# Cross attention of an audio tower: which engine subtracts the maximum from which unit, and ScalarE instructions over two PSUM banks

## The chip, the core and the metric

The kernel runs on one core of a Trainium2 chip. The metric is the device time of one execution in microseconds; the time before is the median of three runs. A core has TensorE (matmuls, from SBUF into PSUM), VectorE, ScalarE and GpSimd, which run side by side, each through its own list of instructions in order, and wait for one another by semaphores. PSUM has banks of 512 fp32 values for each of 128 partitions.

## What is computed

The program is five stages: choice of tokens, retention, a mixture of experts, cross attention, a second mixture of experts. The change touches cross attention alone. Its reference, with 4096 tokens of text (8 batches of 512), 128 videos of 64 frames and 2 heads of 64:

```
q = (text_embeds @ Wq.T + bq).reshape(num_texts, num_words, HEADS, HEAD_DIM)
k = (video_embeds @ Wk.T + bk).reshape(num_vids, num_frames, HEADS, HEAD_DIM)
v = (video_embeds @ Wv.T + bv).reshape(num_vids, num_frames, HEADS, HEAD_DIM)
logits = jnp.einsum('avhd,bthd->abhvt', k, q) / math.sqrt(HEAD_DIM)
weights = jax.nn.softmax(logits, axis=3)
attn = jnp.einsum('avhd,abhvt->abhtd', v, weights)
attn = attn.mean(axis=0)
return attn @ Wo.T + bo
```

The softmax runs over the 64 frames of one video, so every token has one softmax for each of 128 videos and each head.

## The kernel before

Keys and values of all videos are made in the first stage and stay in SBUF. Cross attention then runs over 8 batches (b) x 2 heads (h) x 16 chunks (c), 256 chunks in all, each of 512 keys (8 videos); the chunk's running number is n. A chunk has four units j = 0 to 3, one for each 128 tokens of the batch: a unit is a 128 x 512 tile of logits. Units 0 and 1 are pair 0, units 2 and 3 are pair 1.

What one unit goes through:
- **logits** (lines 1569, 1570): two TensorE matmuls, for the high and the low part of the query, into the unit's own bank of `psL`;
- **maximum** (line 1648): VectorE, one instruction for a pair, gives the negated maxima of 8 videos for each token;
- **shift and exponential**, in one of three ways, which the table `SHIFTED_BY` (line 1518) gives for each j. "TensorE": a matmul adds the negated maxima in PSUM (line 1579), then ScalarE takes the exponential of the whole unit (line 1700). "ScalarE": eight exponentials of 64 columns with the maximum as bias (line 1708). "VectorE": VectorE adds the negated maxima into SBUF (line 1658), then ScalarE takes the exponential in place (line 1703);
- **total** and **invert** (lines 1664, 1670): VectorE, sums of a pair, and reciprocals for the four units of a chunk;
- **normalise** (line 1754): GpSimd multiplies, unit by unit; line 1757 (GpSimd as well) copies the chunk's values, once for each chunk;
- **turning** (line 1589): four TensorE transposes for each unit into bank j % 2 of `psT`, which has two banks;
- **copy** (line 1714): ScalarE copies the turned unit to SBUF, into `turned`;
- **mixing** (line 1602): four matmuls for a chunk (eight records in the trace), which accumulate in `psA` over the 16 chunks of a run (one b and h).

The order on each engine is written out by hand in `step(b, h, c, parity)`, which `steps_of` runs for every chunk on every engine; an engine's step works on several chunks at once. On TensorE the step for chunk n is: logits of pair 0 of n; shift of pair 1 of n - 1; turning of pair 0 of n - 2; mixing of n - 3; shift of pair 0 of n; logits of pair 1 of n; turning of pair 1 of n - 2; and, where c is 1, the projection of the next run's queries (line 1563). On ScalarE: exponentials of pair 1 of n - 1; copies of pair 0 of n - 2; exponentials of pair 0 of n; copies of pair 1 of n - 2. On VectorE: maximum of pair 0 of n; total of pair 1 of n - 1; invert n - 1; maximum of pair 1 of n; subtraction; total of pair 0 of n.

The waits that matter: before the turning of unit j of chunk n TensorE waits until the unit was normalised and until the copy that last read the same bank of `psT` is done (`turned_copied >= 4 * n + j + 1`, which starts at 2). Before it writes a unit's logits it waits for the exponential of the same unit of the chunk before (`exped`). The shift waits for `maxima_ready`. The mixing waits for all four copies of its chunk.

Of the kernel before, what the change touches and what calls it, by code (L numbers as in the profile page):

```python
# [21 lines left out]
ACT = mybir.ActivationFunctionType  # L22
# [3 lines left out]
P = 128  # L26
# [16 lines left out]
SUB = KC // P  # L43
# [1385 lines left out]
def cross_attention(nc, a, K):  # L1429
# [16 lines left out]
    with ExitStack() as ctx:  # L1446
# [10 lines left out]
        with ExitStack() as inner:  # L1457
# [3 lines left out]
            psT = psn("psT", [P, 2, L])  # L1461
            tail_set = sem("tail_set")
            with nc.Block() as block:
                @block.vector
                def _(dve):
                    dve.memset(qT[:, B * L:(B + 1) * L], 0.0).then_inc(tail_set, 1)
                    norm.batches(dve, K.hidden, rows, norm_ready)
# [26 lines left out]
        with ExitStack() as inner:  # L1494
# [5 lines left out]
            weights = sba("weights", [P, WR, KC])  # L1500
            sums, scales = sba("sums", [P, WR, VC]), sba("scales", [P, WR, VC])

            turned = sba("turned", [P, 2, SUB, L])
            chunk_values = sba("chunk_values", [P, 2, SUB, DH1])
            psL, psT = psa("psL", [P, TB, KC]), psa("psT", [P, 2, KC])
# [3 lines left out]
            logits_ready, maxima_ready, exped = sem("logits_ready"), sem("maxima_ready"), sem("exped")  # L1509
            shifted, subtracted = sem("shifted"), sem("subtracted")  # L1510
            summed, scales_ready, normalised = sem("summed"), sem("scales_ready"), sem("normalised")
            turned_ready, turned_copied = sem("turned_ready"), sem("turned_copied")
# [2 lines left out]
            CHUNKS = B * H1 * NKC  # L1515
            LAG = 3

            SHIFTED_BY = ("ScalarE", "TensorE", "VectorE", "TensorE")
            shifted_on = {who: [j for j in range(TB) if SHIFTED_BY[j] == who] for who in set(SHIFTED_BY)}

            def place(j):

                return shifted_on[SHIFTED_BY[j]].index(j) + 1

            def per_chunk(j):
                return len(shifted_on[SHIFTED_BY[j]])

            def steps_of(engine, step):

                def run(b, h):
                    for c in range(4):
                        step(b, h, c, c % 2)
                    with engine.Fori(0, (NKC - 4) // 2) as i:
                        step(b, h, i * 2 + 4, 0)
                        step(b, h, i * 2 + 5, 1)

                for h in range(H1):
                    run(0, h)  # L1540
                with engine.Fori(1, B) as b:
                    for h in range(H1):
                        run(b, h)
                for c in range(LAG):
                    step(B, 0, c, c % 2)

            def index(b, h, c):

                return (b * H1 + h) * NKC + c

            def exists(n):

                return not isinstance(n, int) or 0 <= n < CHUNKS
# [4 lines left out]
            with nc.Block() as block:  # L1558
                @block.tensor
                def _(pe):  # L1560
# [4 lines left out]
                    def logits(n, h, key, j):  # L1565
# [3 lines left out]
                        pe.matmul(psL[:, j, :], q_high[h][:, tile], K.keys[:, ds(key, KC)], start=True, stop=False, skip_group_check=True)  # L1569
                        pe.matmul(psL[:, j, :], q_low[h][:, tile], K.keys[:, ds(key, KC)], start=False, stop=(SHIFTED_BY[j] != "TensorE"),  # L1570
                                  skip_group_check=True).then_inc(logits_ready, 1)

                    def shift(n, pair):

                        units = [j for j in (2 * pair, 2 * pair + 1) if SHIFTED_BY[j] == "TensorE"]
                        if units:
# [61 lines left out]
                def _(dve):  # L1638
# [12 lines left out]
                    def subtract(n, parity, pair, reused):  # L1651
                        for j in (2 * pair, 2 * pair + 1):
                            if SHIFTED_BY[j] == "VectorE":
                                dve.wait_ge(maxima_ready, 2 * n + (pair + 1))
# [34 lines left out]
                @block.scalar  # L1689
                def _(act):  # L1690
                    def high(h, n):
                        act.wait_ge(q_ready, n)
                        act.activation(q_high[h][:], psQ[:], ACT.Identity, bias=K.bq2[:, h:h + 1]).then_inc(q_highs, 1)  # L1693

                    def exponentials(n, parity, pair):
                        for j in (2 * pair, 2 * pair + 1):
                            into = weights[:, 4 * parity + j, :]
                            if SHIFTED_BY[j] == "TensorE":
                                act.wait_ge(shifted, per_chunk(j) * n + place(j))
                                act.activation(into, psL[:, j, :], ACT.Exp).then_inc(exped, 1)  # L1700
                            elif SHIFTED_BY[j] == "VectorE":
                                act.wait_ge(subtracted, per_chunk(j) * n + place(j))
                                act.activation(into, into, ACT.Exp).then_inc(exped, 1)  # L1703
                            else:
                                act.wait_ge(maxima_ready, 2 * n + (pair + 1))
                                for v in range(VC):
                                    video = slice(v * FR, (v + 1) * FR)
                                    ins = act.activation(into[:, video], psL[:, j, video], ACT.Exp, bias=maxima[:, j, v:v + 1].bitcast(F32))  # L1708
                                ins.then_inc(exped, 1)

                    def copy_turned(n, parity, pair):
                        for j in (2 * pair, 2 * pair + 1):
                            act.wait_ge(turned_ready, 4 * n + (j + 1))
                            act.activation(turned[:, parity, :, j * P:(j + 1) * P],  # L1714
                                           psT[:, j % 2, :].rearrange("p (k q) -> p k q", k=SUB), ACT.Copy).then_inc(turned_copied, 1)

                    def keep_run(b, h):

                        act.wait_ge(chunks_mixed, index(b, h, NKC))
                        act.activation(head_sums[h][:, ds(b * L, L)].rearrange("p (side r) -> p side r", side=2),  # L1720
                                       psA[:].rearrange("p (r side) -> p side r", side=2), ACT.Copy,
                                       scale=1.0 / VID).then_inc(run_copied, 1)

                    def step(b, h, c, parity):
                        n = index(b, h, c)
                        early = c if isinstance(c, int) else None
                        if exists(n - 1):
                            exponentials(n - 1, 1 - parity, 1)
                        if exists(n - 2):
                            copy_turned(n - 2, parity, 0)  # L1730
                        if exists(n):
                            exponentials(n, parity, 0)
                        if early == LAG - 1 and exists(n - LAG):
                            if h == 0:
                                keep_run(b - 1, 1)
                            else:
                                keep_run(b, 0)
                        if exists(n - 2):
                            copy_turned(n - 2, parity, 1)
                        if exists(n) and early == 1:  # L1740
                            high(1 - h, b * H1 + h + 2)

                    act.nop().then_inc(run_copied, 1)
                    high(0, 1)
                    steps_of(act, step)
# [83 lines left out]
def audio_tower(nc, a, out):  # L1829

    with ExitStack() as ctx:
        K = Kept(nc, ctx, a)
        select_and_project(nc, a, K)
        retention(nc, a, K)
        route_and_mix(nc, a, K, 1)
        cross_attention(nc, a, K)
        route_and_mix(nc, a, K, 2, out)
# [22 lines left out]
```

## Time and profile before

| | |
|---|---|
| time, median of three runs | 2764.86 us |
| lowest and highest | 2762.68, 2765.0 us |
| span of the profiled execution | 2857.5 us |
| cross attention in that span | 904 to 2478 us, 256 chunks |
| TensorE (matmul), busy | 2308.8 us (81%) |
| VectorE | 2043.2 us (72%) |
| ScalarE | 1794.6 us (63%) |
| GpSimd | 1556.8 us (54%) |

The profile is of one execution of its own; for it there is the span from the first to the last instruction, and no other time. That span is 92.6 us longer than the median of the runs.

The profile's page gives each engine's busy time, the costliest groups of instructions, and what ended the idle time before them. The timeline lists instructions in order of time. PE is TensorE, PEld its weight loads, DVE is VectorE, ACT ScalarE, POOL GpSimd. Matmuls are pipelined: the time from the start of one to the start of the next says what it costs, and its own duration is longer than that.

### The profile page before, as it was taken

To read this page: it belongs to the slowest core of one execution; us is meant where nothing else is said; L and a number is where in the kernel's file an instruction comes from. 1 tells how busy PE (TensorE), PEld (TensorE's weight loads), DVE (VectorE), ACT (ScalarE), POOL (GpSimd) and SP (SyncE) were. 2 spreads that over 40 slices of the span, in tenths; PEclk is the share of its full clock that TensorE was granted. 3 is DMA by queue.
4 is the path that set the end of the run, shared out by engine and by line. 5 is a ranking of instruction groups with operands and counts; after the bars stand their busy time and mean duration, and the time that the engine had idled before them with its cause. 6 is when DMAs were issued, how large, how long until landed. Compare 5 with 4: busy or idle time off the path is not lost. (4 is left out here: it accounts for less than half of the span.)

```text
span 2857.5 us, 49077 instructions
## 1 busy us (share of the span) xinstructions
PE 2308.8 (81%) x12375; PEld 1616.9 (57%) x12376; DVE 2043.2 (72%) x3473; ACT 1794.6 (63%) x5092; POOL 1556.8 (54%) x1661
## 2 busy tenths in 40 slices
PE   4519006776756999999999999999999999857783
PEld 2305005555654666666666666666666666657673
DVE  6811563336017999999999999999999999674554
ACT  2203213221544888888888888888888888605652
POOL 2240560001643776777777777677776777615552
PEclk8755556555886999999999999999999999958987
DMA  6310000003120000000000000000000000041114
GB/s 207 103 33 0 0 0 1 0 0 96 44 60 1 0 0 1 0 0 0 0 0 0 0 0 0 0 0 0 0 0 0 0 0 0 5 106 37 40 38 108
DMA packets 67637, 63.03 MB, mean 22 GB/s; under 512 B 20864, under 2 KB 54656, under 8 KB 67584
## 3 DMA queue, kind: packets, MB, share of 16 engines
q1 hardware_dynamic: 49008, 40.88, 5.1%
q0 software_dynamic: 8192, 16.87, 2.3%
q10 hardware_dynamic: 10384, 4.66, 0.6%
q8 instruction: 23, 0.38, 0.1%
q14 instruction: 30, 0.25, 0.0%
HBM read 48.71 MB, written 13.68 MB: 22 GB/s over the span
## 5 line engine op out<-in xcount | busy, mean ns | idle before, releaser
L1754 POOL TENSOR_TENSOR attend_weights<-attend_weights,attend_scales 128x512 f32<-128x512 f32 x1024 | 1047.1, 1044 | 470.2 <-DVE attend_scales L1670 470.2
L1648 DVE TENSOR_REDUCE attend_maxima<-attend_psL 128x16 fp32r<-128x1024 f32 x512 | 624.2, 1219 | 79.4 <-PE attend_psL L1570 79.4
L1664 DVE TENSOR_REDUCE attend_sums<-attend_weights 128x16 f32<-128x1024 f32 x512 | 618.6, 1208 | 0.1
L1714 ACT ACTIVATE attend_turned<-attend_psT 128x512 f32<-128x512 f32 x1024 | 555.5, 599 | 4.2 <-PE attend_psT L1589 3.8
L1589 PE MATMUL attend_psT<-consts,attend_weights 128*128 128x128 f32 x4096 | 530.5, 272 | 0.8 <-POOL attend_weights L1754 0.8
L1589 PEld LDWEIGHTS attend_psT<-consts,attend_weights 128*128 128x128 f32 x4096 | 477.1, 140 | 69.9 <-POOL attend_weights L1754 2.9
L1602 PE MATMUL attend_psA<-attend_turned,attend_chunk_values 128*64 128x512 f32 x2048 | 495.9, 605 | 0.8 <-ACT attend_turned L1714 0.8
L1708 ACT ACTIVATE attend_weights<-attend_psL,attend_maxima 128x64 f32<-128x64 f32 x2048 | 446.6, 329 | 54.0 <-DVE attend_maxima L1648 54.0
L1569 PE MATMUL attend_psL<-keys,attend_q_high 128*128 (+1 forms) x1024 | 434.5, 424 | 1.6 <-ACT attend_q_high L1693 1.6
L1570 PE MATMUL attend_psL<-keys,attend_q_low 128*128 (+1 forms) x1024 | 404.4, 395 | 0.0
L1700 ACT ACTIVATE attend_weights<-attend_psL 128x512 f32<-128x512 f32 x512 | 314.1, 613 | 0.0
L1703 ACT ACTIVATE attend_weights<-attend_weights 128x512 f32<-128x512 f32 x256 | 161.5, 631 | 134.1 <-DVE attend_weights L1658 134.1
L1602 PEld LDWEIGHTS attend_psA<-attend_turned,attend_chunk_values 128*64 128x64 f32 x2048 | 123.8, 136 | 190.3 <-issue 190.3
L1579 PE MATMUL attend_psL<-attend_maxima,ident_r 128*128 128x512 f32 x512 | 221.1, 432 | 5.4 <-DVE attend_maxima L1648 5.4
L1579 PEld LDWEIGHTS attend_psL<-attend_maxima,ident_r 128*128 128x128 f32 x512 | 95.8, 187 | 224.3 <-DVE attend_maxima L1648 212.5
L1570 PEld LDWEIGHTS attend_psL<-keys,attend_q_low 128*128 128x128 f32 x1024 | 194.8, 190 | 33.0 <-issue 4.1
L1569 PEld LDWEIGHTS attend_psL<-keys,attend_q_high 128*128 128x128 f32 x1024 | 194.2, 190 | 30.9 <-issue 3.6
L1658 DVE TENSOR_TENSOR attend_weights<-attend_psL,attend_maxima 128x512 f32<-128x512 f32 x256 | 177.0, 691 | 35.7 <-DVE attend_maxima L1648 10.1
L1228 POOL DMA_INDIRECT moe2mix_rows<-normed,moe_source x72 | 69.6, 966 | 135.2 <-DVE moe2mix_result L1377 63.3
L904 PE MATMUL decayed_psW<-retention_qkv,decayed_stage 128*128 x48 | 15.9, 434 | 146.4 <-ACT decayed_stage L813 146.2
L157 POOL TENSOR_TENSOR decayed_oroot<-decayed_oms,consts 128x1 f32<-128x1 f32 x32 | 17.3, 541 | 207.5 <-DVE decayed_oms L873 207.5
L1312 ACT ACTIVATE moe2mix_hidT<-moe2mix_psH,moe_b 128x128 f32<-128x128 f32 x288 | 81.9, 369 | 50.9 <-remote 24.6
(317 smaller groups left out, 3004.9 us busy)
## 6 DMA issues: line engine op xcount, KB each, us to landing
select_xbuf<-in_x_dram SPq DMA_DIRECT2D x16, 1024.0 KB
select_emb<-L_attn_video_embeds_dram ACTq DMA_DIRECT2D x16, 256.0 KB
moe2back_back<-result SPq DMA_DIRECT2D x8, 512.0 KB, 7.2
normed<-moe2route_normed SPq DMA_DIRECT2D x4, 520.0 KB, 8.8
moe_w<-in_L_ffn_W_dram SPq DMA_DIRECT2D x1, 2048.0 KB, 10.8
normed<-moe1route_normed SPq DMA_DIRECT2D x4, 512.0 KB, 5.1
moe1back_back<-result SPq DMA_DIRECT2D x4, 512.0 KB, 6.7
moe_w<-in_L_ffn_w_dram SPq DMA_DIRECT2D x1, 2048.0 KB, 11.8
```

The source lines that it names most:

```text
L1569: pe.matmul(psL[:, j, :], q_high[h][:, tile], K.keys[:, ds(key, KC)], start=True, stop=False, skip_group_check=True)
L1570: pe.matmul(psL[:, j, :], q_low[h][:, tile], K.keys[:, ds(key, KC)], start=False, stop=(SHIFTED_BY[j] != "TensorE"), skip_group_check=True ...
L1579: pe.matmul(videos(psL[:, j, :]), K.ident_r[:], maxima[:, j, :, None].to_broadcast([P, VC, FR]), start=False, stop=True, skip_group_check= ...
L1589: mm = pe.matmul(psT[:, j % 2, k * P:(k + 1) * P], weights[:, 4 * parity + j, k * P:(k + 1) * P], ident, is_transpose=True, start=(k == 0) ...
L1602: mm = pe.matmul(psA[part, :], chunk_values[:, parity, k, :], turned[:, parity, k, :], start=(first and k < 2), stop=(k >= SUB - 2), skip_ ...
L1648: dve.tensor_reduce(maxima[:, both, :].rearrange("p j v -> p (j v)"), psL[:, both, :].rearrange("p j (v f) -> p (j v) f", f=FR), X, ALU.ma ...
L1658: dve.tensor_tensor(videos(weights[:, 4 * parity + j, :]), videos(psL[:, j, :]), maxima[:, j, :, None].bitcast(F32).to_broadcast([P, VC, F ...
L1664: dve.tensor_reduce(sums[:, both, :].rearrange("p j v -> p (j v)"), weights[:, both, :].rearrange("p j (v f) -> p (j v) f", f=FR), X, ALU. ...
L1700: act.activation(into, psL[:, j, :], ACT.Exp).then_inc(exped, 1)
L1708: ins = act.activation(into[:, video], psL[:, j, video], ACT.Exp, bias=maxima[:, j, v:v + 1].bitcast(F32))
L1714: act.activation(turned[:, parity, :, j * P:(j + 1) * P], psT[:, j % 2, :].rearrange("p (k q) -> p k q", k=SUB), ACT.Copy).then_inc(turned ...
L1754: pool.tensor_tensor(w, w, scales[:, s, :, None].to_broadcast([P, VC, FR]), ALU.mult).then_inc(normalised, 1)
```

## The change

`SHIFTED_BY` gets another order: units 0 and 1 are now both shifted by TensorE, unit 2 by ScalarE, unit 3 by VectorE. Pair 0 thus has both its units in two neighbouring banks of `psL`, shifted by the same engine, and ScalarE takes their exponentials in one instruction of 1024 columns, which waits for both shifts (`shifted >= 2 * n + 2`) and counts `exped` up by 2 at its end. Pair 1 has the eight small exponentials and the one that follows VectorE's subtraction. The copies of the two turned units of a pair, of pair 0 and of pair 1 alike, become one instruction too, over both banks of `psT`: it waits for the turning of both units and counts `turned_copied` up by 2 at its end.

```diff
-            SHIFTED_BY = ("ScalarE", "TensorE", "VectorE", "TensorE")
+            SHIFTED_BY = ("TensorE", "TensorE", "ScalarE", "VectorE")
...
                     def exponentials(n, parity, pair):
-                        for j in (2 * pair, 2 * pair + 1):
+                        if pair == 0:
+                            act.wait_ge(shifted, 2 * n + 2)
+                            act.activation(weights[:, 4 * parity:4 * parity + 2, :], psL[:, 0:2, :], ACT.Exp).then_inc(exped, 2)
+                            return
+                        for j in (2, 3):
                             into = weights[:, 4 * parity + j, :]
-                            if SHIFTED_BY[j] == "TensorE":
-                                act.wait_ge(shifted, per_chunk(j) * n + place(j))
-                                act.activation(into, psL[:, j, :], ACT.Exp).then_inc(exped, 1)
-                            elif SHIFTED_BY[j] == "VectorE":
+                            if SHIFTED_BY[j] == "VectorE":
...
                     def copy_turned(n, parity, pair):
-                        for j in (2 * pair, 2 * pair + 1):
-                            act.wait_ge(turned_ready, 4 * n + (j + 1))
-                            act.activation(turned[:, parity, :, j * P:(j + 1) * P],
-                                           psT[:, j % 2, :].rearrange("p (k q) -> p k q", k=SUB), ACT.Copy).then_inc(turned_copied, 1)
+                        act.wait_ge(turned_ready, 4 * n + (2 * pair + 2))
+                        act.activation(turned[:, parity, :, 2 * pair * P:(2 * pair + 2) * P].rearrange("p k (j q) -> p j k q", j=2),
+                                       psT[:].rearrange("p j (k q) -> p j k q", k=SUB), ACT.Copy).then_inc(turned_copied, 2)
```

TensorE's list of cross attention, the program before, from the turning of a second pair (the first row) through the next chunk's first logits, shift, turning and mixing to the shift of its first pair:

```order
L1589 MATMUL attend_psT<-consts,attend_weights 128x128 x8
L1569 MATMUL attend_psL<-keys,attend_q_high 128x512
L1570 MATMUL attend_psL<-keys,attend_q_low 128x512
L1569 MATMUL attend_psL<-keys,attend_q_high 128x512
L1570 MATMUL attend_psL<-keys,attend_q_low 128x512
L1579 MATMUL attend_psL<-attend_maxima,ident_r 128x512
L1589 MATMUL attend_psT<-consts,attend_weights 128x128 x8
L1602 MATMUL attend_psA<-attend_turned,attend_chunk_values 64x512 x4
L1579 MATMUL attend_psL<-attend_maxima,ident_r 128x512
```

And the same piece of TensorE's list in the changed program:

```order
L1589 MATMUL attend_psT<-consts,attend_weights 128x128 x8
L1569 MATMUL attend_psL<-keys,attend_q_high 128x512
L1570 MATMUL attend_psL<-keys,attend_q_low 128x512
L1569 MATMUL attend_psL<-keys,attend_q_high 128x512
L1570 MATMUL attend_psL<-keys,attend_q_low 128x512
L1589 MATMUL attend_psT<-consts,attend_weights 128x128 x8
L1602 MATMUL attend_psA<-attend_turned,attend_chunk_values 64x512 x4
L1579 MATMUL attend_psL<-attend_maxima,ident_r 128x512 x2
```

The shift that stood between the first logits and the turning has gone to the shift behind the mixing, where there are now two; the rest stands as it was.

ScalarE's list, the program before, one chunk's step from the exponentials of pair 1 to the copies of pair 1:

```order
L1703 ACTIVATE attend_weights<-attend_weights 128x512
L1700 ACTIVATE attend_weights<-attend_psL 128x512
L1714 ACTIVATE attend_turned<-attend_psT 128x4x128 x2
L1708 ACTIVATE attend_weights<-attend_psL,attend_maxima 128x64 x8
L1700 ACTIVATE attend_weights<-attend_psL 128x512
L1714 ACTIVATE attend_turned<-attend_psT 128x4x128 x2
```

And the same step in the changed program (its lines 1698, 1704 and 1709 are the exponentials):

```order
L1709 ACTIVATE attend_weights<-attend_psL,attend_maxima 128x64 x8
L1704 ACTIVATE attend_weights<-attend_weights 128x512
L1714 ACTIVATE attend_turned<-attend_psT 128x2x4x128
L1698 ACTIVATE attend_weights<-attend_psL 128x1024
L1714 ACTIVATE attend_turned<-attend_psT 128x2x4x128
```

The eight small exponentials went from the first pair to the second, the two exponentials after a shift and each two copies became one instruction. The lists of VectorE and GpSimd have the same rows in the same order; VectorE's subtraction takes unit 3 in place of unit 2.

## Rows read from the trace of the kernel before

**Rows 1.** Busy time by stretch: from:to, length, engines (x instructions), granted clock, DMA.
```profile
core 0: us, PE busy (x) PEld busy (x) DVE busy (x) ACT busy (x) POOL busy (x), PEclk, DMA share, GB/s
...
722.00:842.00 120.00, 90.48 (x660) 82.42 (x659) 11.59 (x40) 68.84 (x230) 71.35 (x74) 0.94 0.16 41
...
904.00:2478.00 1574.00, 1570.78 (x8710) 1036.49 (x8710) 1448.39 (x1543) 1385.62 (x3851) 1120.67 (x1278) 1.00 0.00 0
```
**Rows 2.** Line 1757 (once a chunk): count, least/median/longest ns, first and last start.
```profile
L1757 POOL COPY attend_chunk_values<-values x256: 392/398/400, 910.3 to 2475.3; 128x256 f32 x96, 128x256 f32<-128x256 f32 x32
```
**Rows 3.** Timeline of TensorE over one chunk: start us, duration us, what, xcount.
```profile
1507.98 0.60 PE L1589 MATMUL attend_psT<-consts,attend_weights 128*128 128x128 f32 x4
...
1510.38 0.48 PE L1579 MATMUL attend_psL<-attend_maxima,ident_r 128*128 128x512 f32 x1
1510.70 0.40 PE L1569 MATMUL attend_psL<-keys,attend_q_high 128*128 x1
...
1511.40 0.39 PE L1570 MATMUL attend_psL<-keys,attend_q_low 128*128 x1
1511.63 1.03 PE L1589 MATMUL attend_psT<-consts,attend_weights 128*128 128x128 f32 x8
1512.42 0.48 PE L1569 MATMUL attend_psL<-keys,attend_q_high 128*128 x1
...
1513.44 0.38 PE L1579 MATMUL attend_psL<-attend_maxima,ident_r 128*128 128x512 f32 x1
1513.65 1.04 PE L1589 MATMUL attend_psT<-consts,attend_weights 128*128 128x128 f32 x8
1514.62 1.94 PE L1602 MATMUL attend_psA<-attend_turned,attend_chunk_values 128*64 128x512 f32 x8
1516.49 0.48 PE L1579 MATMUL attend_psL<-attend_maxima,ident_r 128*128 128x512 f32 x1
```
**Rows 4.** Timeline of ScalarE over the same chunk; in brackets idle time and its releaser.
```profile
1510.05 1.75 ACT L1708 ACTIVATE attend_weights<-attend_psL,attend_maxima 128x64 f32<-128x64 f32 x8 [0.17 <-DVE attend_maxima L1648]
1511.63 0.65 ACT L1700 ACTIVATE attend_weights<-attend_psL 128x512 f32<-128x512 f32 x1
1512.26 1.09 ACT L1714 ACTIVATE attend_turned<-attend_psT 128x512 f32<-128x512 f32 x2
1513.90 0.63 ACT L1703 ACTIVATE attend_weights<-attend_weights 128x512 f32<-128x512 f32 x1 [0.55 <-DVE attend_weights L1658]
1514.44 0.58 ACT L1700 ACTIVATE attend_weights<-attend_psL 128x512 f32<-128x512 f32 x1
...
1516.16 0.72 ACT L1708 ACTIVATE attend_weights<-attend_psL,attend_maxima 128x64 f32<-128x64 f32 x3 [0.17 <-DVE attend_maxima L1648]
```
**Rows 5.** Timeline of VectorE over the same chunk.
```profile
1511.83 1.23 DVE L1648 TENSOR_REDUCE attend_maxima<-attend_psL 128x16 fp32r<-128x1024 f32 x1 [0.30 <-PE attend_psL L1570]
1513.17 0.69 DVE L1658 TENSOR_TENSOR attend_weights<-attend_psL,attend_maxima 128x512 f32<-128x512 f32 x1
...
1514.91 1.21 DVE L1648 TENSOR_REDUCE attend_maxima<-attend_psL 128x16 fp32r<-128x1024 f32 x1
1516.04 1.21 DVE L1664 TENSOR_REDUCE attend_sums<-attend_weights 128x16 f32<-128x1024 f32 x1
```
**Rows 6.** Timeline of GpSimd over the same chunk.
```profile
1511.67 2.05 POOL L1754 TENSOR_TENSOR attend_weights<-attend_weights,attend_scales 128x512 f32<-128x512 f32 x2 [1.78 <-DVE attend_scales L1670]
```
**Rows 7.** Timeline at the stage's end, where TensorE waits for ScalarE's last copy.
```profile
2475.56 1.10 PE L1589 MATMUL attend_psT<-consts,attend_weights 128*128 128x128 f32 x8
2476.26 1.08 ACT L1714 ACTIVATE attend_turned<-attend_psT 128x512 f32<-128x512 f32 x2 [1.86 <-PE attend_psT L1589]
...
2477.49 1.94 PE L1602 MATMUL attend_psA<-attend_turned,attend_chunk_values 128*64 128x512 f32 x8 [0.83 <-ACT attend_turned L1714]
```
**Rows 8.** Line 1714, all its instructions: least/median/longest ns, first and last start.
```profile
L1714 ACT ACTIVATE attend_turned<-attend_psT x1024: 586/597/679, 905.3 to 2476.8; 128x512 f32<-128x512 f32 x171
```
**Rows 9.** Line 671, a ScalarE instruction over 1024 elements in another stage.
```profile
L671 ACT ACTIVATE features_t<-retention_qkv x8: 1039/1056/1057, 296.8 to 407.3; 128x1024 f32 x6, 128x1024 f32<-128x1024 f32 x2
```

## The prediction

> **What bounds the kernel now.** Five views were read, from the coarse to the fine. The busy time by stretch [rows 1] says where the change can act: cross attention runs from 904 to 2478 us, 1574 of the 2857.5 us of the profiled span, and in it the granted clock is 1.00, TensorE's 2.4 GHz, with 1570.78 us of matmul busy. That last number alone proves nothing, since pipelined matmuls overlap, so the timeline of TensorE over one chunk comes next [rows 3]. Take the start of the first pair's shift as the clock of a chunk. It stands at 1510.38 and again at 1516.49: 6.11 us. The instruction that is issued once per chunk agrees: the 256 copies of values start from 910.3 to 2475.3, so 1565.0 / 255 = 6.14 us [rows 2]. 256 chunks of 6.14 us are the stage.
>
> Inside the 6.11 us every TensorE group starts where the one ahead lets it: four logits in 0.93 us (1510.70 to 1511.63), transposes 0.11 us apart ((1.03 - 0.60) / 4), the mixing in 1.87 us (1514.62 to 1516.49) [rows 3]. Is it ever late for somebody? The maximum that the shift at 1516.49 needs is a VectorE row of 1514.91 + 1.21 = 1516.12 [rows 5], 0.37 us early. The copies that free the two banks of psT end at 1512.26 + 1.09 = 1513.35 [rows 4], and the turning that overwrites them starts at 1513.65 with its first bank and 0.43 us later with its second; the first bank's copy, 0.60 us long [rows 8], ended at 1512.86. So 0.8 us of slack for the first bank. The weights come from GpSimd by 1511.67 + 1.02 and + 2.05 [rows 6], also early. TensorE is dense and is the bound; ScalarE (88% of the stage) waits 0.55 us before its exponential of the VectorE unit [rows 4], and VectorE (92%) 0.30 us [rows 5]. What can make the stage longer is a new wait of TensorE; what only relieves ScalarE gives nothing.
>
> **The change part by part.** *Exponentials of pair 0, one instruction over two banks.* The two 512-element exponentials from PSUM cost 0.65 and 0.58 us [rows 4]. A 1024-element instruction isn't in this stage. In another stage one takes 1056 ns [rows 9], against 632 for 512 from SBUF (the 0.63 row in [rows 4]), so 512 elements more cost 0.43 us. For the exponential: 0.65 + 0.43 = 1.08 us. It needs both shifts. In the chunk's clock these stand at 0 and 0.32 us (the distance from a shift to the next matmul, 1510.38 to 1510.70); the second ends at 0.32 + 0.38, the exponential runs from about 0.74 to 1.82. Its readers, VectorE's sums and the next logits, come later than that. Cost: nothing.
>
> *The ScalarE unit moved to pair 1, the VectorE unit to place 3.* Eight exponentials (1.75 us) and one (0.63 us) now follow each other, 2.3 us in all. VectorE's subtraction is the same length. They start when the copy worked out below has been issued, near 3.5 us of the chunk's clock, and end near 5.7. VectorE asks for them when its next maximum is through: that one starts at 4.53 now (1510.38 to 1514.91), 0.21 us later after the change (see below), and the row behind it 1.13 us after that (1514.91 to 1516.04), at 5.87 us. Thin, and hidden. Both shifts now stand ahead of logits 2 and 3. TensorE's work is the same, but VectorE's second maximum starts 0.21 us later (one shift, 1513.44 to 1513.65 [rows 3]). The next chunk's first maximum then ends at 4.53 + 0.21 + 1.21 = 5.95 us, still before the next shift. By itself this part costs nothing.
>
> *Copies of a pair as one instruction.* Here a wait appears. Before, the first bank was copied while TensorE filled the second. Now the copy waits for both and frees both only at its end; what is queued behind TensorE's wait is the turning of the next chunk's first pair, the mixing, the shifts, the logits, everything. And between the two turnings on that side stood four logits and a shift; the shift has moved away. Worked out from the shift at 0:
> - second pair's turning starts at 1.25 (1510.38 to 1511.63) + 0.21 for the second shift = 1.46;
> - its eight transposes end at 1.46 + 1.03 = 2.49 [rows 3];
> - handoff to ScalarE, 0.04 (a logit ends at 1511.40 + 0.39, VectorE starts at 1511.83 [rows 3, 5]): 2.53, when ScalarE has been free since 1.82;
> - the copy, 0.60 (median of 512 elements [rows 8]) + 0.43 = 1.03: 3.56;
> - handoff back, 0.15 (at the stage's end the last copy ends at 2476.26 + 1.08 and the mixing that waits for it starts at 2477.49 [rows 7]): 3.71;
> - restart: transposes after a wait took 1.10 instead of 1.03 [rows 7], + 0.07;
> - turning and mixing up to the next shift, 1513.65 to 1516.49: 2.84.
>
> Sum 6.62 us, against 6.11 now: 0.51 us more. The same by the cover: the next turning follows 0.79 + 1.02 us after the start of this one (1511.63 to 1512.42 to 1513.44), so 0.78 us after its end, while 0.04 + 1.03 + 0.15 + 0.07 = 1.29 are needed. With the shift still between, the cover would have been 0.99 and the stall 0.30; so of 0.51 us some 0.21 belongs to the pair of edits together.
>
> The other copy (first pair) has no such race: it starts when pair 1's exponentials are issued, at 3.5 + 2.1 = 5.6 us, ends near 6.6, and is wanted at 6.62 + 1.46 = 8.1.
>
> There are 255 passages from one chunk to the next. In 16 of them the queries' projection (two matmuls of 0.59 us) stands between, which covers the stall. 239 x 0.51 = 122 us. **Bounds of the unknowns.** The copy: from 1.03 to twice 0.60 = 1.20, if two banks cost as two instructions; I take 1.03, since the 1056 ns row is the nearest. The handoff and restart: from 0.04 + 0 (VectorE to ScalarE, 1514.91 + 1.21 to 1516.16 [rows 4, 5]) to 0.22; I take 0.22, because its row is this very pair of instructions. Low end: 0.51 - 0.18 = 0.33 us, 79 us. High end: 0.51 + 0.17 = 0.68 us, 163 us.
>
> The Trainium skill ("ScalarE: Activation LUTs", section "What ACT_TABLE_LOAD costs") puts an ACTIVATE with immediate operands at 186 ns plus 0.833 ns an element, 613 for 512 and 1039 for 1024; the rows say 597 and 1056, so by the page the total would come out within 3 us of the same.
>
> The span and the times: 2857.5 us is the profiled span, 92.6 us above the median of 2764.86, and no time of that execution is given apart from its span. The dense TensorE period has no room for a profiler's share, so I add the 122 us to either: 2980 for a profiled span and **2887 us** for the median.
>
> **The rivals.** *Faster: ScalarE was the bound.* Its 88% speaks for it. Per chunk the change saves it two fixed parts of copies (1.09 - 1.03 each) and one of exponentials (1.23 - 1.08), 0.27 us: 69 us, 2696 us. It would decide only if a TensorE instruction waited for ScalarE today; the slack of 0.8 us in [rows 3, 4] and the rows of ScalarE waiting speak against. 6%. The Trainium skill, same page and section, says that back-to-back ACTIVATEs overlap by about 93 ns; two copies of 0.60 that take 1.09 together show it here, and it makes the saving smaller still.
>
> *Same: no new wait decides.* The stall vanishes if handoffs, restart and copy fit in 0.78 us, so if the 1024-element copy took 0.6 us at most, or if TensorE's write of one bank were let go before the instruction ends. One increment stands on the copy's end, so only the first is open, and 1056 ns speaks against it. 2765 us, 7%.
>
> *Slower by the clock.* The new stall is an idle piece of half a microsecond in each chunk. From 722 to 842 us TensorE was busy for 90.48 of 120 us and the clock granted was 0.94 [rows 1]; the stage then takes another 1574 x (1 / 0.94 - 1) = 100 us, 2987 us. Speaking against: TensorE would still be busy for some 92% of each chunk. 4%. The Trainium skill ("TensorE: Matmul & The Clock Gate", section "A second HAM failure mode: psum-queue depth-cycling") describes a kernel whose short idles between matmul groups made the clock go up and down; by that rule this rival would happen, and [rows 1] bear out only a small part of it.
>
> **How the numbers follow.** The stall as worked out: 83%, from 2764.86 + 79 = 2844 to 2764.86 + 163 = 2928. The rivals hold the remaining 17%, so this case's range is the range: 2844 to 2928. A median of this kernel can be told from no change at about 0.2%, 5.5 us. Slower 83 + 4 = 87%, same 7%, faster 6%.
>
> **What would show it.** In the profile after: shift to shift 6.6 us in place of 6.11; TensorE idle before L1589 in each chunk, put down to ScalarE's copy; the copies as 512 rows of about 1.03 us; VectorE's idle time before its second maximum longer; granted clock 1.00. Wrong would be: a period of 6.1 with an idle ScalarE (the cover was longer than thought), a copy far from 1.03 us, a handoff of 0.04, or the stall in front of another row, above all VectorE's sums waiting for pair 1's exponentials, where only 0.2 us was left.

## The result

| | before | changed |
|---|---|---|
| time, median | 2764.86 us | 2892.16 us |
| span of the profiled execution | 2857.5 us | 2924.5 us |
| first to last copy of values (once a chunk) | 1565.0 us | 1690.4 us |
| the same for one chunk, / 255 | 6.137 us | 6.629 us |

The changed kernel takes 1.0452 times as long, with a 95% interval of 1.0427 to 1.0476: 4.5% slower, 127.3 us between the medians. Executions of all kernels here, the one before too, differ by some 40 us in stages ahead of cross attention (the same part of the retention stage took 56 us in one profile, at a granted clock of 0.90, and 94 us in that of the kernel before and that of the changed kernel, at 0.50), so what follows compares the length of the cross-attention stage, and never two spans.

By that measure the stage grew by 1690.4 - 1565.0 = 125.4 us, all of the 127.3 us but 2. Line 1757 in the changed kernel, as [rows 2]:

```profile
L1757 POOL COPY attend_chunk_values<-values x256: 393/398/404, 881.4 to 2571.8; 128x256 f32 x96, 128x256 f32<-128x256 f32 x32
```

The busy time of that stretch, which answers to [rows 1] (the columns are those there):

```profile
881.00:2572.00 1691.00, 1607.23 (x8670) 1014.14 (x8668) 1443.06 (x1537) 1318.24 (x3079) 1119.45 (x1275) 1.00 0.00 0
```

TensorE is busy for 1607 of 1691 us, 95%, where before no gap showed; the granted clock is 1.00 as before. So it isn't the clock: the array stands still for a part of each chunk. The timeline of TensorE over one chunk, as [rows 3], says where, and in brackets for whom:

```profile
1522.94 0.70 PE L1579 MATMUL attend_psL<-attend_maxima,ident_r 128*128 128x512 f32 x2
...
1524.40 1.03 PE L1589 MATMUL attend_psT<-consts,attend_weights 128*128 128x128 f32 x8
1525.19 0.48 PE L1569 MATMUL attend_psL<-keys,attend_q_high 128*128 x1
...
1525.98 0.40 PE L1570 MATMUL attend_psL<-keys,attend_q_low 128*128 x1
1526.71 1.06 PE L1589 MATMUL attend_psT<-consts,attend_weights 128*128 128x128 f32 x8 [0.33 <-ACT attend_turned L1714]
1527.70 1.94 PE L1602 MATMUL attend_psA<-attend_turned,attend_chunk_values 128*64 128x512 f32 x8
1529.57 0.70 PE L1579 MATMUL attend_psL<-attend_maxima,ident_r 128*128 128x512 f32 x2
```

And ScalarE over the same chunk, as [rows 4]:

```profile
1523.73 1.03 ACT L1698 ACTIVATE attend_weights<-attend_psL 128x1024 f32<-128x1024 f32 x1 [0.73 <-PE attend_psL L1579]
1525.54 1.03 ACT L1714 ACTIVATE attend_turned<-attend_psT 128x1024 f32<-128x1024 f32 x1 [0.77 <-PE attend_psT L1589]
1526.46 1.74 ACT L1709 ACTIVATE attend_weights<-attend_psL,attend_maxima 128x64 f32<-128x64 f32 x8
1528.03 0.69 ACT L1704 ACTIVATE attend_weights<-attend_weights 128x512 f32<-128x512 f32 x1
```

Read the two together. Shift to shift is 1522.94 to 1529.57, 6.63 us. The turning of pair 1 starts at 1524.40 and ends at 1525.43; ScalarE had been waiting for it and copies from 1525.54 to 1526.57; TensorE's last logits started at 1525.98, and the next turning, which would have followed at 1526.21, starts at 1526.71. ScalarE and TensorE now wait for each other in turn. The groups on the page say how often:

```profile
L1714 ACT ACTIVATE attend_turned<-attend_psT 128x1024 f32<-128x1024 f32 x512 | 540.1, 1055 | 193.3 <-PE attend_psT L1589 193.3
...
L1589 PE MATMUL attend_psT<-consts,attend_weights 128*128 128x128 f32 x4096 | 537.0, 274 | 83.8 <-ACT attend_turned L1714 83.6
L1589 PEld LDWEIGHTS attend_psT<-consts,attend_weights 128*128 128x128 f32 x4096 | 459.1, 140 | 218.3 <-POOL attend_weights L1754 178.1
```

Two things to learn from these rows. First, 83.6 us of waiting are not the loss: the idle time of PE is counted from the modelled end of a matmul (1525.98 + 0.40), not from the point where the next could have started (0.23 us after its start), so 0.33 us stand where 0.50 are lost. Second, the weight loads of the same line are put down to GpSimd (178.1 us), though GpSimd had been done for long:

```profile
1523.86 2.05 POOL L1754 TENSOR_TENSOR attend_weights<-attend_weights,attend_scales 128x512 f32<-128x512 f32 x2 [1.91 <-DVE attend_scales L1670]
```

Its first unit was ready near 1524.9 and its second at 1525.9, the turning came at 1526.71. Before the turning stand two waits, for `normalised` and for `turned_copied`; the end of ScalarE's copy at 1526.57 is the one that fits.

### The profile page after: what moved, and what is told of

Same layout as the page of the kernel before. It is cut to its first block and busy times, and to the rows that moved or that the text cites. A ratio compares the mean times of both kernels' runs of the same rounds, so it can differ in the third digit from the quotient of the medians.

```text
span 2924.5 us, 48097 instructions
## 1 busy us (share of the span) xinstructions
PE 2319.4 (79%) x12375; PEld 1571.3 (54%) x12376; DVE 2046.4 (70%) x3473; ACT 1733.3 (59%) x4324; POOL 1559.5 (53%) x1661
## 5 line engine op out<-in xcount | busy, mean ns | idle before, releaser
L1714 ACT ACTIVATE attend_turned<-attend_psT 128x1024 f32<-128x1024 f32 x512 | 540.1, 1055 | 193.3 <-PE attend_psT L1589 193.3
L1589 PE MATMUL attend_psT<-consts,attend_weights 128*128 128x128 f32 x4096 | 537.0, 274 | 83.8 <-ACT attend_turned L1714 83.6
L1589 PEld LDWEIGHTS attend_psT<-consts,attend_weights 128*128 128x128 f32 x4096 | 459.1, 140 | 218.3 <-POOL attend_weights L1754 178.1
L1698 ACT ACTIVATE attend_weights<-attend_psL 128x1024 f32<-128x1024 f32 x256 | 263.1, 1028 | 189.3 <-PE attend_psL L1579 189.3
L1579 PEld LDWEIGHTS attend_psL<-attend_maxima,ident_r 128*128 128x128 f32 x512 | 76.5, 188 | 211.9 <-DVE attend_maxima L1648 211.9
L1579 PE MATMUL attend_psL<-attend_maxima,ident_r 128*128 128x512 f32 x512 | 180.0, 433 | 4.9 <-DVE attend_maxima L1648 4.9
L1704 ACT ACTIVATE attend_weights<-attend_weights 128x512 f32<-128x512 f32 x256 | 176.2, 688 | 0.0
L1228 POOL DMA_INDIRECT moe2mix_rows<-normed,moe_source x72 | 69.8, 969 | 104.2 <-SPq L1224 50.9
L904 PEld LDWEIGHTS decayed_psW<-retention_qkv,decayed_stage 128*128 128x128 f32 x48 | 14.8, 318 | 166.4 <-issue 166.4
```

Source lines behind the costliest of these rows:

```text
L1579: pe.matmul(videos(psL[:, j, :]), K.ident_r[:], maxima[:, j, :, None].to_broadcast([P, VC, FR]), start=False, stop=True, skip_group_check= ...
L1589: mm = pe.matmul(psT[:, j % 2, k * P:(k + 1) * P], weights[:, 4 * parity + j, k * P:(k + 1) * P], ident, is_transpose=True, start=(k == 0) ...
L1698: act.activation(weights[:, 4 * parity:4 * parity + 2, :], psL[:, 0:2, :], ACT.Exp).then_inc(exped, 2)
L1714: act.activation(turned[:, parity, :, 2 * pair * P:(2 * pair + 2) * P].rearrange("p k (j q) -> p j k q", j=2), psT[:].rearrange("p j (k q) ...
```

## The experiments

The theory is the prediction's: a race between the copy of pair 1 and the TensorE work that stands between the turning of pair 1 and the next turning. The rivals are that the new order of the units costs by itself (rival 1), and that an instruction over two banks does (rival 2). Every stage length below is that of the once-a-chunk copy of values, first to last start, as [rows 2].

**One part at a time: the order of the units alone.**

```diff
-            SHIFTED_BY = ("ScalarE", "TensorE", "VectorE", "TensorE")
+            SHIFTED_BY = ("TensorE", "TensorE", "ScalarE", "VectorE")
```

> The kernel before with the new order of the units alone: units 0 and 1 shifted by TensorE, 2 by ScalarE, 3 by VectorE, but every exponential and every copy still an instruction of its own. Theory (the long copy of pair 1 makes TensorE wait): the period stays at 6.11 to 6.14 us a chunk, 2765 us. Rival 1 (the shift that has left the place between the first logits and the turning, or the eight small exponentials in pair 1, cost time by themselves): 0.2 to 0.5 us a chunk, 2815 to 2890 us.

```profile
L1757 POOL COPY attend_chunk_values<-values x256: 393/397/403, 884.5 to 2452.0; 128x256 f32 x96, 128x256 f32<-128x256 f32 x32
```

1567.5 us, 2.5 more than before; the lowest time was 2764.62 us beside 2762.09 of the kernel before. By itself, with all copies apart, moving the shift and the eight small exponentials is next to free. Rival 1 has fallen.

**The long copies alone, in the old order.**

```diff
-                        for j in (2 * pair, 2 * pair + 1):
-                            act.wait_ge(turned_ready, 4 * n + (j + 1))
-                            act.activation(turned[:, parity, :, j * P:(j + 1) * P],
-                                           psT[:, j % 2, :].rearrange("p (k q) -> p k q", k=SUB), ACT.Copy).then_inc(turned_copied, 1)
+                        act.wait_ge(turned_ready, 4 * n + (2 * pair + 2))
+                        act.activation(turned[:, parity, :, 2 * pair * P:(2 * pair + 2) * P].rearrange("p k (j q) -> p j k q", j=2),
+                                       psT[:].rearrange("p j (k q) -> p j k q", k=SUB), ACT.Copy).then_inc(turned_copied, 2)
```

> The kernel before with each two copies as one instruction, and nothing else: the old order of the units, the exponentials apart. Theory: the shift still stands between the two turnings, so the cover is 0.99 us against 1.29 us needed; the stall is 0.30 us in 239 chunks, 72 us, 2837 us, and TensorE is shown waiting for line 1714. Rival 1 (the order of the units is what costs): 2765 us. Rival 2 (reading two banks at once disturbs TensorE or VectorE, whatever the cover): about as much as the whole change, 2885 us.

```profile
L1756 POOL COPY attend_chunk_values<-values x256: 391/396/400, 842.7 to 2480.8; 128x256 f32 x96, 128x256 f32<-128x256 f32 x32
```

1638.1 us, 73.1 more than before, where 72 were expected; the ratio of the times is 1.0267 (1.0248 to 1.0286). The wait sits where it should, but one part of the expectation missed: the profile shows no wait for the copy. TensorE's timeline:

```profile
1506.01 0.40 PE L1570 MATMUL attend_psL<-keys,attend_q_low 128*128 x1
1506.24 0.38 PE L1579 MATMUL attend_psL<-attend_maxima,ident_r 128*128 128x512 f32 x1
1506.74 1.07 PE L1589 MATMUL attend_psT<-consts,attend_weights 128*128 128x128 f32 x8
```

From the shift to the turning there are 0.50 us where [rows 3] have 0.21. The gap is there, 0.29 us in each chunk: 0.17 of it lie inside the 0.38 us that the row of the shift lasts, and no idle time is listed for the 0.12 that remain. The distance between starts is what to read. The loss does leave a mark in the rows of TensorE's weight loads for the turning, though with the wrong name beside it. Between 1000 and 2360 us of this profile (waited for, us in total, times, longest):

```profile
PEld attend_psT L1589 <- POOL attend_weights L1753: 101.0, 198, 0.5
```

The same view of the kernel before has no row for that line. ScalarE's copy in that chunk, 1505.57 to 1506.60, ends 0.14 us ahead of the turning:

```profile
1505.57 1.03 ACT L1713 ACTIVATE attend_turned<-attend_psT 128x1024 f32<-128x1024 f32 x1 [0.78 <-PE attend_psT L1589]
```

**Which of the two copies: pair 1 apart again.** The changed kernel, but the long copy only for pair 0.

```diff
+                        if pair == 0:
+                            act.wait_ge(turned_ready, 4 * n + (2 * pair + 2))
...
+                            return
+                        for j in (2 * pair, 2 * pair + 1):
+                            act.wait_ge(turned_ready, 4 * n + (j + 1))
+                            act.activation(turned[:, parity, :, j * P:(j + 1) * P],
+                                           psT[:, j % 2, :].rearrange("p (k q) -> p k q", k=SUB), ACT.Copy).then_inc(turned_copied, 1)
```

> The changed kernel with the copies of pair 1 apart again; the copies of pair 0 and the exponentials of pair 0 stay single instructions over two banks. Theory: only the copy of pair 1 stands between two turnings, so all of the loss is gone: 6.11 to 6.14 us a chunk, 2765 us. Rival 2 (instructions over two banks cost time as such): about half of the loss stays, 2825 us.

```profile
L1763 POOL COPY attend_chunk_values<-values x256: 392/397/410, 887.7 to 2455.3; 128x256 f32 x96, 128x256 f32<-128x256 f32 x32
```

1567.6 us: the whole loss is gone, with the other two long instructions still in place. The ratio of the times is 0.9926 (0.9852 to 0.9999), whose width comes from the stages ahead; the lowest times are 2764.83 us and, before, 2762.09. So the time that ScalarE saves on the exponentials and the copy of pair 0 buys nothing either.

**And pair 0 apart again**, with the long copy only for pair 1 (the condition of the edit above turned round).

> The changed kernel with the copies of pair 0 apart again; the copy of pair 1 stays one instruction. Theory: the copy of pair 0 has more than 1 us of slack either way, so nothing is won back: 6.63 us a chunk, 2885 to 2892 us. Rival 2: about half is won back, 2825 us.

```profile
L1763 POOL COPY attend_chunk_values<-values x256: 392/396/403, 846.4 to 2538.3; 128x256 f32 x96, 128x256 f32<-128x256 f32 x32
```

1691.9 us, as slow as the changed kernel (1690.4); the ratio of the times is 1.0347 (1.0274 to 1.0421). The loss belongs to one of the three merged instructions alone. Rival 2 has fallen: it is the same instruction over the same two banks that costs nothing for pair 0.

**What in the long copy: its late start or its late end?** Two copies for a pair again, first with both banks freed at the end of the second:

```diff
-                        act.wait_ge(turned_ready, 4 * n + (2 * pair + 2))
...
+                        for j in (2 * pair, 2 * pair + 1):
+                            act.wait_ge(turned_ready, 4 * n + (j + 1))
+                            ins = act.activation(turned[:, parity, :, j * P:(j + 1) * P],
+                                                 psT[:, j % 2, :].rearrange("p (k q) -> p k q", k=SUB), ACT.Copy)
+                        ins.then_inc(turned_copied, 2)
```

> The changed kernel with two copies for each pair, of which the first starts as soon as its own bank is turned, but both banks are freed only at the end of the second. Theory, by the same sum: the first copy starts at 2.10 us of the chunk's clock, the second at 2.59 and ends at 3.19, with 0.22 us of handoff and restart 3.41 against 3.27 for an unhindered turning: 0.14 us a chunk, 33 us, 2798 us. If freeing both at the end is what costs, and not the late start: near 2885 us.

then with both waiting for both units, and each freeing its own bank:

```diff
                         act.wait_ge(turned_ready, 4 * n + (2 * pair + 2))
...
+                        for j in (2 * pair, 2 * pair + 1):
+                            act.activation(turned[:, parity, :, j * P:(j + 1) * P],
+                                           psT[:, j % 2, :].rearrange("p (k q) -> p k q", k=SUB), ACT.Copy).then_inc(turned_copied, 1)
```

> The changed kernel with two copies for each pair that both wait for both units to be turned, each freeing its own bank at its end. Theory: the first copy runs from 2.53 to 3.13 us of the chunk's clock, the turning of the first bank starts at 3.35 against 3.27; the second ends at 3.62, which is 3.77 to 3.84 with the handoff against 3.78: 0.08 to 0.14 us a chunk, 19 to 33 us, 2784 to 2798 us. If the late start alone is what costs: near 2885 us.

The first row is that of both banks freed at the end, the second that of the late start:

```profile
L1759 POOL COPY attend_chunk_values<-values x256: 392/396/401, 903.5 to 2503.0; 128x256 f32 x96, 128x256 f32<-128x256 f32 x32
```

```profile
L1758 POOL COPY attend_chunk_values<-values x256: 393/396/403, 863.7 to 2449.6; 128x256 f32 x96, 128x256 f32<-128x256 f32 x32
```

1599.5 and 1585.9 us: 34.5 and 20.9 us more than before, where 33 and 19 to 33 were expected. The first of these agreements is partly luck. In the profile with both banks freed at the end, six passages from one chunk to the next, each 32 chunks after the last, take 7.74 to 7.83 us and not 6.20, 9.5 us in all. In each of them ScalarE stands idle for 2.2 us ahead of the eight small exponentials, for which the profile names no releaser. Between 1000 and 2360 us of it (us in total, times, longest):

```profile
ACT attend_weights L1709 <- issue: 13.1, 6, 2.2
```

Where this comes from is open. The other passages take 6.20 us: the race costs 0.09 us a chunk there, where 0.14 were expected. With the late start they take 6.19 us, 0.08 a chunk, the low end of the 0.08 to 0.14 expected. So neither half explains the loss, nor do the two add up to it: 55.4 us against 125.4, or 0.17 against 0.52 a chunk. That is how a race behaves: each half first eats slack, and only what is left over shows. The times say less than the stage lengths (ratios 1.0221, 1.0088 to 1.0355, and 1.0111, 0.9931 to 1.0290): the lowest time of the first is 73.8 us above that of the kernel before, of which 34.5 lie in this stage.

**The dose: shorter copies.** The changed kernel with copies of 768 and of 512 elements, by a cut of the innermost range of both operands (`[:, :, :, 0:96]` and `[:, :, :, 0:64]`). What they leave out of the turned weights stays at zero.

> The changed kernel whose copies of a pair take 96 of every 128 columns, 768 elements in place of 1024 (the other columns of the turned weights are left out, they stay at zero from a GpSimd memset ahead of the stage, which adds some 5 us). Theory: the copy is 0.21 us shorter and so is the stall, 0.51 - 0.21 = 0.30 us a chunk, 72 us, 2837 us, with the memset 2842 us. If the number of waits or handoffs matters and not the copy's length: near 2890 us.

> The same with 64 of every 128 columns, 512 elements. Theory: 0.43 us shorter, the stall 0.08 us a chunk, 19 us, 2784 us, with the memset 2789 us. If the number of waits or handoffs matters and not the copy's length: near 2890 us.

768 elements, then 512, each with the row of line 1719, the copy, and of line 1762, the once-a-chunk copy of values:

```profile
L1719 ACT ACTIVATE attend_turned<-attend_psT x512: 811/818/871, 863.9 to 2508.5; 128x768 f32<-128x768 f32 x171
```

```profile
L1762 POOL COPY attend_chunk_values<-values x256: 397/398/403, 867.9 to 2507.1; 128x256 f32 x96, 128x256 f32<-128x256 f32 x32
```

```profile
L1719 ACT ACTIVATE attend_turned<-attend_psT x512: 597/602/659, 859.7 to 2453.5; 128x512 f32<-128x512 f32 x171
```

```profile
L1762 POOL COPY attend_chunk_values<-values x256: 395/398/407, 863.8 to 2452.1; 128x256 f32 x96, 128x256 f32<-128x256 f32 x32
```

| copy | its median | stage | more than before | expected |
|---|---|---|---|---|
| 1024 (the changed kernel) | 1.03 us | 1690.4 us | 125.4 us | 122 us |
| 768 | 0.82 us | 1639.2 us | 74.2 us | 72 us |
| 512 | 0.60 us | 1588.3 us | 23.3 us | 19 us |

From 1024 to 768 elements the copy is 0.21 us shorter and the stage 51.2 us, from 768 to 512 again 0.22 and 50.9 us: 0.21 and 0.21 us for each of 239 chunks. A nanosecond of the copy is a nanosecond of the chunk. The times of these two are wide (ratios 1.0292, 1.0046 to 1.0538, and 1.0116, 0.9872 to 1.0360); the lowest, 2897.29 and 2841.04 us, are 79.6 and 23.4 us above the 2817.67 of the kernel before beside them, in line with the stage lengths.

**An order with more cover.** The long way between the two turnings of a chunk and the next suggests another order: TensorE turns pair 1 right after the mixing, with the units in the changed kernel's order and every exponential and copy apart.

```diff
-            SHIFTED_BY = ("ScalarE", "TensorE", "VectorE", "TensorE")
+            SHIFTED_BY = ("TensorE", "TensorE", "ScalarE", "VectorE")
...
+                        if exists(n - 2):
+                            turn_weights(n - 2, parity, 1)
                         if exists(n):
                             shift(n, 0)
                             for j in (2, 3):
                                 logits(n, h, key, j)
-                        if exists(n - 2):
-                            turn_weights(n - 2, parity, 1)
...
+                        if exists(n - 2):
+                            copy_turned(n - 2, parity, 0)
                         if exists(n - 1):
                             exponentials(n - 1, 1 - parity, 1)
-                        if exists(n - 2):
-                            copy_turned(n - 2, parity, 0)
```

> Not a part of the change: an order that gives the copies more cover, to see whether it can beat the kernel before. New order of the units, all instructions apart, TensorE turns pair 1 right behind the mixing, ahead of the shifts, and ScalarE copies pair 0 ahead of the exponentials of pair 1. TensorE then changes once less in a chunk between kinds of matmul (about 0.1 us each by the distances in the timeline), so if TensorE stays dense: 6.0 us a chunk, 2740 us. Rival: the copy of pair 1 now stands behind both exponentials of pair 0 on ScalarE, or VectorE's next maximum comes too late, and a wait of TensorE takes the gain: 6.2 to 6.6 us a chunk, 2790 to 2890 us.

```profile
L1757 POOL COPY attend_chunk_values<-values x256: 393/398/404, 845.0 to 2703.4; 128x256 f32 x96, 128x256 f32<-128x256 f32 x32
```

It is the slowest of all: 1858.4 us of stage, 7.29 a chunk, ratio 1.1064 (1.0869 to 1.1258). The wait is neither of the two that were named. TensorE, ScalarE, VectorE and GpSimd, one row each:

```profile
1509.15 0.66 PE L1589 MATMUL attend_psT<-consts,attend_weights 128*128 128x128 f32 x4 [0.35 <-POOL attend_weights L1754]
```

```profile
1509.85 0.60 ACT L1714 ACTIVATE attend_turned<-attend_psT 128x512 f32<-128x512 f32 x1 [0.40 <-PE attend_psT L1589]
```

```profile
1512.63 1.22 DVE L1664 TENSOR_REDUCE attend_sums<-attend_weights 128x16 f32<-128x1024 f32 x1 [1.56 <-ACT attend_weights L1703]
```

```profile
1514.38 2.04 POOL L1754 TENSOR_TENSOR attend_weights<-attend_weights,attend_scales 128x512 f32<-128x512 f32 x2 [2.94 <-DVE attend_scales L1670]
```

The copy of pair 0 stands ahead of the exponentials of pair 1 on ScalarE; so these wait for the turning, the sums for them, GpSimd for the reciprocals, and the turning of the next pair 0 (1516.47, 7.32 us after 1509.15) for GpSimd. One swap on ScalarE closed a ring through four engines. That the turning had more cover was worth nothing beside it. Here the row that names GpSimd is right: its second unit is ready at 1514.38 + 2.04 = 1516.42. The same order on TensorE with ScalarE's old order wasn't tried.

## Why the prediction was right

The forecast was 2887 us and 0.51 us a chunk; measured were 2892.16 us and 0.52 us, 125.4 us of stage against 122. Its steps, in the chunk's clock:

| step | predicted | in the chunk at 1522.94 |
|---|---|---|
| turning of pair 1 starts | 1.46 | 1524.40, 1.46 |
| its eight transposes | 1.03 | 1.03 |
| handoff to ScalarE | 0.04 | 1525.43 to 1525.54, 0.11 |
| the copy | 1.03 | 1.03 |
| handoff back | 0.15 | 1526.57 to 1526.71, 0.14 |
| restart, turning, mixing, up to the next shift | 2.91 | 1526.71 to 1529.57, 2.86 |
| sum | 6.62 | 6.63 |

- What bounds the kernel: TensorE, dense, with ScalarE at 88% not the bound. Shown by the changed kernel with pair 1 apart: ScalarE has two instructions fewer in each chunk than before, and the stage isn't shorter (1567.6 against 1565.0 us).
- The exponentials of pair 0 and the move of the units cost nothing: shown within 2.5 us (the order alone) and 2.6 us (with the exponentials merged). The exponential takes 1.03 us, not 1.08. The 2.5 us aren't spread over all chunks: with the order alone, 41 passages from one mixing to the next take 6.18 to 6.20 us, while most others take 6.10; what TensorE waits for in the 41 is open. The narrow spot that the prediction named, VectorE's sums waiting for pair 1's exponentials, has 1.0 us of idle time in the whole page of the changed kernel: it held, and narrowly. In the chunk at 1522.94 these exponentials end at 1528.72 and the sums start at 1528.82, so 0.1 us of room was left, where the prediction had 0.2.
- The copy of pair 0 has slack: shown, since keeping it long or short changes the stage by 1.5 us.
- The division of the loss, 0.30 us with the old cover and 0.21 more for the shift that left it: measured 73.1 us and 125.4 - 73.1 = 52.3 us, or 0.31 and 0.22 for each of 239 chunks.
- The count, 239 stalls, was off by one: the first of the 16 projections stands ahead of the first mixing, so 15 of the 255 passages have one, and the trace puts 240 waits of TensorE down to this copy. That the projection covers the stall is shown: those 15 take 6.96 us before and 6.96 to 6.98 after.
- Two terms were off, by little and in opposite directions. The handoff from TensorE to ScalarE is 0.11 us behind transposes, where the row taken was one from a 512-column matmul to VectorE. The restart after a wait costs 0.02 to 0.03 us (the eight transposes take 1.06 in place of 1.03), where the row from the stage's end gave 0.07. One was 0.07 us too low and the other 0.05 too high; that the sum comes within 0.01 us of the measured one is luck to that extent. What the sum had right was the row for the way back, 0.15 us from ScalarE's copy to TensorE: it was the same pair of instructions.
- The faster rival (ScalarE as the bound) and the rival of no change fell with the same rows. The rival by the clock fell too: granted 1.00 over the whole stage, with an idle piece in each chunk. So by these rows the rule of the Trainium skill on matmul groups with short idles between them ("TensorE: Matmul & The Clock Gate", section "A second HAM failure mode: psum-queue depth-cycling") doesn't reach this case, at 0.5 us lost of 6.63. The price of an ACTIVATE with immediate operands in the Trainium skill ("ScalarE: Activation LUTs", section "What ACT_TABLE_LOAD costs") gives an estimate of 1039 ns for 1024 elements. Measured are 1032 ns (least 1024) for the copy and 1027 for the exponential: the trace agrees.
- In the faster rival, the overlap of two copies was counted twice: the 1.09 us of [rows 4] for a pair of them has it already, so it doesn't make the saving of 0.06 smaller still. No chance rested on it.

## What to carry to other kernels

Two buffers that are filled one after the other and emptied one after the other are a pipeline of two; one instruction that empties both turns them into one buffer, and the writer waits for the last of the filling, the whole emptying and two handoffs, unless it has that much other work in between. So before merging instructions across buffers, add up the producer's work between the end of one filling and the next and hold it against the merged instruction's length plus the handoffs: here 0.78 us against 1.28 (0.11 + 1.03 + 0.14). And ask whose time the merge saves: where another engine is dense, the saved overhead of an 88% busy one is worth nothing, and every nanosecond by which the dense one is made to wait is paid in full.

## What the runs showed of the hardware

A ScalarE instruction over two PSUM banks costs what its elements cost: 1.03 us for 1024, 0.82 for 768, 0.60 for 512 (0.43 us for 512 more), while TensorE writes other banks. The second bank hardly adds a price of its own: 512 elements from two banks take 602 ns, from one bank 597 [rows 8]. From the end of transposes to the start of a waiting ScalarE instruction went 0.11 us, from its end to the start of the waiting transposes 0.14 us; so a pair of handoffs is a quarter of the copy itself. And a wait of 0.3 us in each chunk can leave no idle time in the rows of TensorE's matmuls, as with the long copies in the old order, where 73 us were lost: it shows in the distances between starts, and in the rows of the weight loads, there under the name of an engine that had long been done.
